# Cross attention: one preparation piece per key tile, keys split bank by bank

## The chip, the cores and the metric

The kernel runs on one core of a Trainium2 chip, as one program. TensorE (PE) multiplies and writes to PSUM, eight banks of 512 f32 columns. VectorE (DVE) and ScalarE (ACT) read PSUM; GpSimd (POOL) works on SBUF; SyncE (SP) issues all DMAs, from one queue in order. Each engine executes its own list of instructions in order, and they wait for each other only at semaphores. The metric is the device time of one execution in microseconds (us). The kernel before took 6407.64 us in the median of three runs (6407.46 to 6416.72).

## The reference

The input is x (32 batches of 100 tokens, 128 wide), a condition vector per batch and a context of 1444 tokens per batch. Four layers follow each other. Layers 0, 1 and 3 are transformer blocks (self attention, cross attention over the context, MLP); layer 2 is a routed mixture without these phases. The change is in the cross attention of layers 0, 1 and 3. In layer 0 the context is normalized first:

```python
q_c = _ln(x) @ W_qc + b_qc
kv_c = _ln(context) @ W_kvc + b_kvc          # layers 1 and 3: context as it is
k_c, v_c = jnp.split(kv_c, 2, axis=-1)
# 16 heads, 8 wide
c_attn_w = jax.nn.softmax(jnp.einsum('bhqd,bhsd->bhqs', q_c, k_c) * scale, axis=-1)
c_attn_out = jnp.einsum('bhqs,bhsd->bhqd', c_attn_w, v_c)
x = x + c_attn_out.transpose(0, 2, 1, 3).reshape(B, N, H) @ W_cproj + b_cproj
```

## The kernel before

`cross_attention_phase` (L934) is a software pipeline over 32 batches. Its unit is a slot: in the slot of batch k, PE computes the scores and the values of batch k, the row maxima of batches k+1 and k+2 and the preparation of batches k+2 and k+3, and the queues carry batches ahead of and behind it. All engines run the same slots, from -3 to 31; slots 1 to 24 are a loop. The order of each engine is written out by hand.

A slot has 12 key tiles, kt 0 to 11, of 128 context tokens (the last has 36). For each key tile PE (`pe_slot`, L1116) does in this order:

- the scores of the tile, two halves of four matmuls (`pe_scores`, L1084, matmul L1093). The queries and keys were split in three bf16 parts, and a row with the negated row maximum is part of the product. ACT turns each half into probabilities (`act_exp`, L1175, activation L1182). A half waits until the exponentials of two halves earlier are done.
- two maxima matmuls (`pe_max`, L1059, matmul L1072) into two banks of the ring; DVE reduces each to one column (`dve_max`, L1216, L1227). There are 48 maxima tiles in a slot, numbered x = 4 kt to 4 kt + 3: the first 32 are for batch k+1, the last 16 for batch k+2.
- the values of the tile before, 16 matmuls of f32 that the trace shows as 32 (`pe_values`, L1097, L1110). The accumulator is copied out once per slot by DVE (`dve_out`, L1253, L1256), after maximum 2.
- two more maxima.
- in kt 8 the turn (`pe_turn_max`, L1075, L1082): the row maxima are transposed, and DVE makes the negated maxima in three parts from them (`dve_negmax`, L1236, L1244 to L1251); SP sends them into the query stack (`sp_negmax`, L1340).
- the preparation pieces that the table `PREPS` (L955) puts in this tile. T0 to T2 transpose the context (L1044), K0 to K2 multiply it with the key weights (L1049), V0 to V2 with the value weights (L1055). Each piece fills one bank, and ACT copies it out (`act_prep`, L1137), behind the exponentials of the same tile: to `ctxT` (L1148), `kf` (L1154), `vals` (L1160, L1165).

Maxima, turn and pieces share a ring of three PSUM banks. `ring_tables` (L913) gives each a place in the order in which PE writes them, and PE waits before it writes to a bank until what was in it has been read (`pe_ring_free`, L1009). One place is left out ahead of the turn and one ahead of maximum 46.

When K2 has been copied, POOL splits the keys in three bf16 parts, with four instructions over all 1444 columns (`pool_split_keys`, L1295, L1302 to L1308). SP then writes the parts to a DRAM stack (`sp_keys_out`, L1349), and two slots ahead of its scores a batch's stack is loaded (`sp_stacks`, L1326). SP's order in a slot is: stack and queries, context (`sp_load_ctx`), sums out (`sp_out`), negated maxima, keys out.

In layer 0 (`normed`) three things are added for batch k+4: DVE takes the statistics of one context tile behind each of the maxima 4 to 15 (`dve_stats`, L1202), aggregates them behind maximum 40 (`dve_aggregate`, L1210) and takes the reciprocal behind maximum 45 (`dve_ctx_rstd`, L1214); ACT takes the square root at the end of kt 10 (`act_ctx_std`, L1173), which needs another table than the exponential; POOL normalizes the context behind the split of the keys (`pool_norm`, L1281).

Of the kernel before, what the change touches and what calls it, by code (L numbers as in the profile page):

```python
# [7 lines left out]
ALU = mybir.AluOpType  # L8
# [5 lines left out]
S = 1444  # L14
# [5 lines left out]
BANK = 512  # L20
# [913 lines left out]
def cross_attention_phase(g, wk, kb, wv, normed):  # L934
# [17 lines left out]
    KW = 16 * 2 * len(K_RUNS)  # L952
    Q_SLOTS = ((0, 3), (3, 2), (5, 1))

    PREPS = {1: ("V0", "V1"), 2: ("V2", "T0"), 3: ("T1", "T2"), 4: ("K0",), 5: ("K1", "K2")}  # L955
    PREP_INDEX = {"T0": 0, "T1": 1, "T2": 2, "K0": 3, "K1": 4, "K2": 5, "V0": 6, "V1": 7, "V2": 8}
    ring_of = lambda kt: ([4 * kt, 4 * kt + 1, 4 * kt + 2, 4 * kt + 3] + (["turn"] if kt == TURN_KT else [])
                          + list(PREPS.get(kt, ())))
# [3 lines left out]
    with ExitStack() as st:  # L962
# [174 lines left out]
        def act_prep(slot, name):  # L1137
            k, i = prep_batch(slot, name), int(name[1])
            if k is None:
                return  # L1140
            b, s, r = k.b, k.s, k.r
            act = g.act
            wait(act, p_full, S1 * b + PREP_INDEX[name] + 1)
            at = bank_of(name)
            if name[0] == "T":
                a = BANK * i
                w = min(BANK, S - a)
                nc.scalar.activation(ctxT[:, a:a + w], ps[:, at:at + w], ACT.Copy).then_inc(p_read, 1)  # L1148
            elif name[0] == "K":
                if i == 0:  # L1150
                    wait(act, parts_ready, b)
                a = BANK * i
                w = min(BANK, S - a)
                nc.scalar.activation(kf[:, a:a + w], ps[:, at:at + w], ACT.Identity, bias=kb).then_inc(p_read, 1)  # L1154
            else:
                k0 = 4 * i
                if i == 0:
                    wait(act, pv_done, KT * (b - LAG + 1))
                full = 4 if i < 2 else 3
                ins = nc.scalar.activation(vals[s][:, k0:k0 + full, :, 0:HD],  # L1160
                                           ps[:, at:at + 128 * full].rearrange("p (k h d) -> p k h d", k=full, h=HEADS),
                                           ACT.Copy)
# [95 lines left out]
        def dve_slot(slot):  # L1258
            before, k1, k4 = slot.k(-1), slot.k(1), slot.k(4)
            for x in range(MT):  # L1260
                dve_max(slot, x)
                if x == 2 and before is not None:
                    dve_out(before)
                if x == MT - MAX_A - 1 and k1 is not None:
                    dve_rowmax(k1)
                if x == 4 * TURN_KT + 3 and k1 is not None:
                    dve_negmax(k1)
                if normed and k4 is not None:
                    if 4 <= x < 4 + KT:
# [22 lines left out]
                nc.gpsimd.tensor_tensor(ctok[s][0:n, last, :], ctok[s][0:n, last, :],  # L1292
                                        column[0:n, last, :].to_broadcast([n, P]), op).then_inc(ctx_ready, 1)

        def pool_split_keys(k):  # L1295

            b, s, r = k.b, k.s, k.r
            pool = g.pool
            wait(pool, p_read, S1 * b + PREP_INDEX["K2"] + 1)
            p = k.prev()  # L1300
            wait(pool, k_written[p.s], KW * (p.r + 1))
            pool_copy(parts[:, 0, :], kf[:, :]).then_inc(split, 1)  # L1302
            wait(pool, split, 3 * b + 1)
            nc.gpsimd.tensor_tensor(kf[:, :], kf[:, :], parts[:, 0, :], ALU.subtract).then_inc(split, 1)  # L1304
            wait(pool, split, 3 * b + 2)
            pool_copy(parts[:, 1, :], kf[:, :]).then_inc(split, 1)
            wait(pool, split, 3 * b + 3)
            nc.gpsimd.tensor_tensor(parts[:, 2, :], kf[:, :], parts[:, 1, :], ALU.subtract).then_inc(parts_ready, 1)  # L1308
# [738 lines left out]
```

## Time and profile before

| what | value |
|---|---|
| median of the runs (lowest, highest) | 6407.64 us (6407.46, 6416.72) |
| profiled execution: time | 6396.8 us |
| profiled execution: span of the core | 6395.0 us |
| mean granted clock of TensorE | 0.866 |
| PE busy over the span | 5146.5 us, 80% |
| PEld (weight loads) | 3314.4 us, 52% |
| DVE | 4097.1 us, 64% |
| ACT | 2978.6 us, 47% |
| POOL | 1581.0 us, 25% |
| maxima L1227 | 2719.1 us busy, 889.9 idle before |
| exponentials L1182 | 1800.9 us busy, 654.2 idle before |

The shares are means over phases with different limits. The execution that was profiled took 6396.8 us, below the lowest of the three timed runs; durations of rows are to be summed against it. Busy time of PE is modelled from the start of matmuls that overlap, so neighbours in the rows overlap. In the rows below, "idle before" in brackets is the time in which the engine had nothing to do before the instruction, and the name behind the arrow is what ended it. A row of the timeline merges neighbours of one kind (xN).

### The profile page before, as it was taken

To read this page: it belongs to the slowest core of one execution; us is meant where nothing else is said; L and a number is where in the kernel's file an instruction comes from. 1 tells how busy PE (TensorE), PEld (TensorE's weight loads), DVE (VectorE), ACT (ScalarE), POOL (GpSimd) and SP (SyncE) were. 2 spreads that over 40 slices of the span, in tenths; PEclk is the share of its full clock that TensorE was granted. 3 is DMA by queue.
4 is the path that set the end of the run, shared out by engine and by line. 5 is a ranking of instruction groups with operands and counts; after the bars stand their busy time and mean duration, and the time that the engine had idled before them with its cause. 6 is when DMAs were issued, how large, how long until landed. Compare 5 with 4: busy or idle time off the path is not lost. (4 is left out here: it accounts for less than half of the span.)

```text
span 6395.0 us, 151199 instructions
## 1 busy us (share of the span) xinstructions
PE 5146.5 (80%) x63886; PEld 3314.4 (52%) x63886; DVE 4097.1 (64%) x7828; ACT 2978.6 (47%) x4342; POOL 1581.0 (25%) x869
## 2 busy tenths in 40 slices
PE   3837999999964839999999757779575699999996
PEld 2614555555542615666666435555352366666663
DVE  5546888888855527777777642324455477777784
ACT  1323666666642315666666522212222366666663
POOL 2024444444312032233222110000301322322221
PEclk7657999999986659999999877769765799999998
DMA  3425555555403434555555111110151555555540
GB/s 72 69 45 161 161 162 162 162 162 162 148 7 63 70 106 156 169 163 162 168 170 171 51 27 51 47 38 1 37 83 28 151 178 168 163 163 172 171 130 15
DMA packets 559421, 726.21 MB, mean 114 GB/s; under 512 B 195354, under 2 KB 471994, under 8 KB 546362
## 3 DMA queue, kind: packets, MB, share of 16 engines
q1 hardware_dynamic: 547226, 701.17, 37.8%
q10 hardware_dynamic: 11520, 15.37, 1.0%
q8 instruction: 505, 8.27, 0.5%
q14 instruction: 170, 1.39, 0.1%
HBM read 450.42 MB, written 264.09 MB: 112 GB/s over the span
## 5 line engine op out<-in xcount | busy, mean ns | idle before, releaser
L1227 DVE TENSOR_REDUCE maxima<-ps 100x1 f32<-100x482 f32 (+1 forms) x4608 | 2719.1, 649 | 889.9 <-PE ps L1072 880.3
L1182 ACT ACTIVATE probs<-ps 128x800 f32<-128x800 f32 (+1 forms) x2304 | 1800.9, 835 | 654.2 <-PE ps L1093 652.5
L1072 PE MATMUL ps<-kst,qst 48*100 48x482 bf16 (+1 forms) x4608 | 1114.3, 410 | 107.9 <-DMA qst<-cross_q_parts 51.5
L1279 POOL TENSOR_TENSOR kparts<-kf,zero 128x1444 bf16<-128x1444 f32 x192 | 498.3, 2595 | 2273.9 <-ACT kf L1154 2243.9
L1110 PE MATMUL ps<-probs,vals 128*9 128x100 f32 x36864 | 1012.5, 250 | 7.9 <-ACT probs L1182 0.8
L1093 PE MATMUL ps<-qst,kst 128*128 128x200 bf16 (+1 forms) x9216 | 999.6, 250 | 10.6 <-DMA qst<-nparts 4.3
L1093 PEld LDWEIGHTS ps<-qst,kst 128*128 128x128 bf16 (+1 forms) x9216 | 759.0, 98 | 250.3 <-issue 124.9
L1110 PEld LDWEIGHTS ps<-probs,vals 128*9 128x9 f32 x36864 | 734.3, 90 | 259.7 <-issue 219.3
L1072 PEld LDWEIGHTS ps<-kst,qst 48*100 48x100 bf16 x4608 | 341.1, 119 | 627.5 <-DVE maxima L1227 328.4
L1160 ACT ACTIVATE vals<-ps 128x512 f32<-128x512 f32 (+1 forms) x288 | 162.1, 563 | 465.8 <-PE ps L1055 465.8
L1044 PE MATMUL ps<-ident,ctok 128*128 128x128 f32 (+1 forms) x1152 | 194.6, 290 | 213.8 <-DMA ctok<-in_ctx_dram 110.1
L711 ACT ACTIVATE probs<-ps 100x800 f32<-100x800 f32 x192 | 159.6, 837 | 368.5 <-PE ps L659 367.5
L1154 ACT ACTIVATE kf<-ps,perm_b_L 128x512 f32<-128x512 f32 (+1 forms) x288 | 190.4, 662 | 285.4 <-PE ps L1049 272.4
L1049 PE MATMUL ps<-ctxT,perm_wk_L 128*128 128x512 f32 (+1 forms) x576 | 288.4, 611 | 39.6 <-DVE maxima L1227 29.5
L723 DVE TENSOR_REDUCE maxima<-ps 100x4 f32<-100x400 f32 x384 | 205.4, 570 | 140.9 <-PE ps L637 140.0
L1304 POOL TENSOR_TENSOR kf<-kf,kparts 128x1444 f32<-128x1444 f32 x96 | 283.2, 2950 | 7.5
L1308 POOL TENSOR_TENSOR kparts<-kf,kparts 128x1444 bf16<-128x1444 f32 x96 | 282.8, 2946 | 7.6
L1044 PEld LDWEIGHTS ps<-ident,ctok 128*128 128x128 f32 (+1 forms) x1152 | 127.0, 143 | 295.7 <-issue 216.3
L1148 ACT ACTIVATE ctxT<-ps 128x512 f32<-128x512 f32 (+1 forms) x288 | 164.7, 572 | 228.8 <-PE ps L1044 225.4
L637 PE MATMUL ps<-kst 96*100 96x100 bf16 x1152 | 143.7, 288 | 152.8 <-DMA kst<-k_parts 124.8
L1055 PE MATMUL ps<-wkv_L,ctxT 128*128 128x128 f32 (+1 forms) x1536 | 217.9, 289 | 32.0 <-DVE maxima L1227 30.5
L1055 PEld LDWEIGHTS ps<-wkv_L,ctxT 128*128 128x128 f32 (+1 forms) x1536 | 181.3, 189 | 76.9 <-DVE maxima L1227 65.6
(251 smaller groups left out, 5193.9 us busy)
## 6 DMA issues: line engine op xcount, KB each, us to landing
kst<-ctx_k_stack SPq DMA_DIRECT2D x96, 2888.0 KB
ctx_k_stack<-kparts SPq DMA_DIRECT2D x192, 541.5 KB
ctx_k_stack<-kparts SPq DMA_DIRECT2D x192, 361.0 KB
ctok<-in_ctx_dram SPq DMA_DIRECT2D x96, 704.0 KB
ctx_k_stack<-kparts SPq DMA_DIRECT2D x192, 180.5 KB
c<-in_ctx_dram SPq DMA_DIRECT2D x32, 704.0 KB
o_sums<-osb SPq DMA_DIRECT2D x96, 200.0 KB
qst<-cross_q_parts SPq DMA_DIRECT2D x1152, 12.5 KB
```

What stands on the lines that cost most here:

```text
L723: nc.vector.tensor_reduce(maxima[:, t // 4, c:c + 4], ps[0:N, at:at + CH].rearrange("p (h k) -> p h k", h=4), AX.X, ALU.max).then_inc(m_re ...
L1044: ins = nc.tensor.transpose(ps[:, at + 128 * q:at + 128 * q + n], ctok[s][0:n, kt, :], g.ident[0:n, 0:n])
L1049: ins = nc.tensor.matmul(ps[:, at:at + w], wk, ctxT[:, a:a + w], start=True, stop=True)
L1055: ins = nc.tensor.matmul(ps[0:n, at + 128 * q:at + 128 * q + 128], ctxT[:, 128 * kt:128 * kt + n], wv, start=True, stop=True)
L1072: nc.tensor.matmul(ps[0:N, at:at + w], g.qst[s][row0:row0 + CROWS, j, N * e:N * e + N], g.kst[s][row0:row0 + CROWS, j, a:a + w], start=Tru ...
L1093: ins = nc.tensor.matmul(ps[0:kts[kt], o:o + 2 * N], g.kst[s][0:KROWS, 4 * hf + jj, 128 * kt:128 * kt + kts[kt]], g.qst[s][0:KROWS, 4 * hf ...
L1110: ins = nc.tensor.matmul(ps[q:q + VW, o:o + N], vals[s][:, kt, h, :], probs[kt % 2][hf][:, N * (2 * jj + e):N * (2 * jj + e) + N], start=( ...
L1182: nc.scalar.activation(probs[kt % 2][hf][0:kts[kt], :].rearrange("p (k n) -> p k n", k=2), src, ACT.Exp).then_inc(exp_done, 1)
L1227: nc.vector.reduce_max(maxima[:, col:col + 1], ps[0:N, at:at + widths[c]], AX.X).then_inc(m_read, 1)
L1279: return nc.gpsimd.tensor_tensor(out, src, g.zero[0:src.shape[0], 0:1].to_broadcast(list(src.shape)), ALU.add)
L1304: nc.gpsimd.tensor_tensor(kf[:, :], kf[:, :], parts[:, 0, :], ALU.subtract).then_inc(split, 1)
L1308: nc.gpsimd.tensor_tensor(parts[:, 2, :], kf[:, :], parts[:, 1, :], ALU.subtract).then_inc(parts_ready, 1)
```

## The change

The table `PREPS` puts one piece in each of kt 0 to 7 and one in kt 9, in the same order V, T, K, so the order in which pieces follow each other on PE and ACT is the same. A constant `STD_KT` of 6 puts the square root of layer 0 at the end of kt 6, the aggregation behind maximum 20 and the reciprocal behind maximum 28. The split of the keys works on one bank (512, 512 and 420 columns) as soon as it is copied: twelve instructions in the place of four. The semaphore counts follow; SP's order stays, and keys go out when all three banks are split.

```diff
@@ cross_attention_phase
-    PREPS = {1: ("V0", "V1"), 2: ("V2", "T0"), 3: ("T1", "T2"), 4: ("K0",), 5: ("K1", "K2")}
+    PREPS = {0: ("V0",), 1: ("V1",), 2: ("V2",), 3: ("T0",), 4: ("T1",), 5: ("T2",), 6: ("K0",), 7: ("K1",), 9: ("K2",)}
+    STD_KT = 6
@@ act_prep, K pieces
-                    wait(act, parts_ready, b)
+                    wait(act, parts_ready, 3 * b)
@@ act_slot
-                if kt == KT - 2 and normed and k4 is not None:
+                if kt == STD_KT and normed and k4 is not None:
                     act_ctx_std(k4)
@@ dve_slot
-                    if x == MT - 8:
+                    if x == 4 * STD_KT - 4:
                         dve_aggregate(k4)
-                    if x == MT - 3:
+                    if x == 4 * STD_KT + 4:
                         dve_ctx_rstd(k4)
@@ pool_split_keys
-        def pool_split_keys(k):
+        def pool_split_keys(k, i):
...
-            wait(pool, p_read, S1 * b + PREP_INDEX["K2"] + 1)
-            p = k.prev()
-            wait(pool, k_written[p.s], KW * (p.r + 1))
-            pool_copy(parts[:, 0, :], kf[:, :]).then_inc(split, 1)
...
+            wait(pool, p_read, S1 * b + PREP_INDEX["K0"] + i + 1)
+            if i == 0:
+                p = k.prev()
+                wait(pool, k_written[p.s], KW * (p.r + 1))
+            a = BANK * i
+            z = min(a + BANK, S)
+            done = 9 * b + 3 * i
+            pool_copy(parts[:, 0, a:z], kf[:, a:z]).then_inc(split, 1)
+            wait(pool, split, done + 1)
+            nc.gpsimd.tensor_tensor(kf[:, a:z], kf[:, a:z], parts[:, 0, a:z], ALU.subtract).then_inc(split, 1)
...
@@ pool_slot
-                pool_split_keys(k3)
+                for i in range(3):
+                    pool_split_keys(k3, i)
@@ sp_keys_out
-            wait(sp, parts_ready, b + 1)
+            wait(sp, parts_ready, 3 * (b + 1))
```

Lines behind the table are numbered one higher in the changed kernel. The first place is PE in layer 0, kt 0 and kt 1 of a slot: L1093 are scores, L1072 maxima, L1110 values, L1055 V pieces. Before:

```order
L1093 MATMUL ps<-qst_11,kst_11 128x200 x8
L1072 MATMUL ps<-kst_11,qst_11 100x480 x2
L1110 MATMUL ps<-probs_90,vals_90 9x100 x16
L1072 MATMUL ps<-kst_11,qst_11 100x482 x2
L1093 MATMUL ps<-qst_11,kst_11 128x200 x8
L1072 MATMUL ps<-kst_11,qst_11 100x482 x2
L1110 MATMUL ps<-probs_90,vals_90 9x100 x16
L1072 MATMUL ps<-kst_11,qst_11 100x480 x2
L1055 MATMUL ps<-wkv_L,ctxT 128x128 x8
```

And after:

```order
L1094 MATMUL ps<-qst_11,kst_11 128x200 x8
L1073 MATMUL ps<-kst_11,qst_11 100x480 x2
L1111 MATMUL ps<-probs_90,vals_90 9x100 x16
L1073 MATMUL ps<-kst_11,qst_11 100x482 x2
L1056 MATMUL ps<-wkv_L,ctxT 128x128 x4
L1094 MATMUL ps<-qst_11,kst_11 128x200 x8
L1073 MATMUL ps<-kst_11,qst_11 100x482 x2
L1111 MATMUL ps<-probs_90,vals_90 9x100 x16
L1073 MATMUL ps<-kst_11,qst_11 100x480 x2
L1056 MATMUL ps<-wkv_L,ctxT 128x128 x4
```

V0 and V1 stood together behind kt 1; now V0 stands behind the last maxima of kt 0 and V1 behind those of kt 1.

The second place is PE behind the turn, kt 9 (L1082 is the turn). Before:

```order
L1082 MATMUL ps<-ident,rowmax 16x100
L1093 MATMUL ps<-qst_11,kst_11 128x200 x8
L1072 MATMUL ps<-kst_11,qst_11 100x480 x2
L1110 MATMUL ps<-probs_90,vals_90 9x100 x16
L1072 MATMUL ps<-kst_11,qst_11 100x482 x2
L1093 MATMUL ps<-qst_11,kst_11 128x200 x8
```

And after:

```order
L1083 MATMUL ps<-ident,rowmax 16x100
L1094 MATMUL ps<-qst_11,kst_11 128x200 x8
L1073 MATMUL ps<-kst_11,qst_11 100x480 x2
L1111 MATMUL ps<-probs_90,vals_90 9x100 x16
L1073 MATMUL ps<-kst_11,qst_11 100x482 x2
L1050 MATMUL ps<-ctxT,perm_wk_L 128x420
L1094 MATMUL ps<-qst_11,kst_11 128x200 x8
```

K2 came from kt 5 to the tile behind the turn.

The third place is ACT in layer 0, from the copy of K0 on (L1154, in kf): L1182 are exponentials, two for each key tile, and L1173 is the square root. Before:

```order
L1154 ACTIVATE kf<-ps,perm_b_L 128x512
L1182 ACTIVATE probs_90<-ps 128x800 x2
L1154 ACTIVATE kf<-ps,perm_b_L 128x512
L1154 ACTIVATE kf<-ps,perm_b_L 128x420
L1182 ACTIVATE probs_90<-ps 128x800 x10
L1173 ACT_TABLE_LOAD
L1173 ACTIVATE rstd<-meanvar,eps 128x12
L1182 ACT_TABLE_LOAD
L1182 ACTIVATE probs_90<-ps 36x800 x2
```

And after:

```order
L1155 ACTIVATE kf<-ps,perm_b_L 128x512
L1174 ACT_TABLE_LOAD
L1174 ACTIVATE rstd<-meanvar,eps 128x12
L1183 ACT_TABLE_LOAD
L1183 ACTIVATE probs_90<-ps 128x800 x2
L1155 ACTIVATE kf<-ps,perm_b_L 128x512
L1183 ACTIVATE probs_90<-ps 128x800 x4
L1155 ACTIVATE kf<-ps,perm_b_L 128x420
L1183 ACTIVATE probs_90<-ps 128x800 x2
L1183 ACTIVATE probs_90<-ps 36x800 x2
```

The square root with its two table loads stood between the exponentials of kt 10 and kt 11; now it stands between the copy of K0 and the exponentials of kt 7.

## Rows read from the trace of the kernel before

**Rows 1.** One line's instructions, L1256, in layers 0 and 1: times, first and last start

```profile
L1256 DVE COPY osb<-ps x28: 562/564/566, 603.4 to 1692.8; 128x400 f32<-128x400 f32 x28
L1256 DVE COPY osb<-ps x29: 562/565/566, 2466.5 to 3542.1; 128x400 f32<-128x400 f32 x29
```

**Rows 2.** Busy time by window, one layer 1 slot: PE, PEld, DVE, ACT, POOL, clock, DMA

```profile
3004.20:3042.60 38.40, 36.50 (x574) 23.92 (x571) 29.56 (x55) 23.78 (x35) 11.10 (x4) 1.00 0.54 169
```

**Rows 3.** Timeline of PE in that slot, from kt 1: start us, us, instruction

```profile
3003.54 0.86 PE L1093 MATMUL ps<-qst,kst 128*128 128x200 bf16 x8
...
3008.42 0.85 PE L1093 MATMUL ps<-qst,kst 128*128 128x200 bf16 x8
...
3012.62 0.85 PE L1093 MATMUL ps<-qst,kst 128*128 128x200 bf16 x8
...
3016.35 0.86 PE L1093 MATMUL ps<-qst,kst 128*128 128x200 bf16 x8
...
3018.86 1.12 PE L1049 MATMUL ps<-ctxT,perm_wk_L 128*128 128x512 f32 x2 [0.17 <-DVE maxima L1227]
3019.83 0.85 PE L1093 MATMUL ps<-qst,kst 128*128 128x200 bf16 x8
...
3024.00 0.85 PE L1093 MATMUL ps<-qst,kst 128*128 128x200 bf16 x8
...
3028.55 0.86 PE L1093 MATMUL ps<-qst,kst 128*128 128x200 bf16 x8
...
3032.15 0.25 PE L1082 MATMUL ps<-ident,rowmax 100*16 100x100 f32 x1 [0.82 <-DVE maxima L1227]
3032.23 0.85 PE L1093 MATMUL ps<-qst,kst 128*128 128x200 bf16 x8
...
3039.67 0.86 PE L1093 MATMUL ps<-qst,kst 128*128 128x200 bf16 x8
```

**Rows 4.** Timeline of DVE in that slot: kt 4, kt 8, behind the negated maxima

```profile
3017.59 2.36 DVE L1227 TENSOR_REDUCE maxima<-ps 100x1 f32<-100x482 f32 x4 [1.38 <-PE ps L1072]
...
3030.21 2.36 DVE L1227 TENSOR_REDUCE maxima<-ps 100x1 f32<-100x482 f32 x4
...
3033.52 6.92 DVE L1227 TENSOR_REDUCE maxima<-ps 100x1 f32<-100x480 f32 x12
```

**Rows 5.** Timeline of PE in slot 29 of layer 1 (no T, no K)

```profile
3546.28 0.85 PE L1093 MATMUL ps<-qst,kst 128*128 128x200 bf16 x8
...
3549.98 0.86 PE L1093 MATMUL ps<-qst,kst 128*128 128x200 bf16 x8
...
3553.64 0.41 PE L1072 MATMUL ps<-kst,qst 48*100 48x482 bf16 x2 [0.52 <-DVE maxima L1227]
```

**Rows 6.** Timeline of DVE in a slot of layer 0: statistics and aggregation

```profile
1013.03 0.28 DVE L1202 BATCH_NORM_STATS2 stats<-ctok 128x6 f32<-128x128 f32 x1
1013.23 0.64 DVE L1227 TENSOR_REDUCE maxima<-ps 100x1 f32<-100x482 f32 x1
...
1039.84 0.80 DVE L1210 BATCH_NORM_AGGREGATE meanvar<-stats 128x2 f32<-128x6 f32 x11
```

**Rows 7.** Timeline of ACT: table loads of layer 0; copy of K0 in layer 1

```profile
1040.07 1.28 ACT L1173 ACT_TABLE_LOAD   x1
...
1042.98 3.09 ACT L1182 ACTIVATE probs<-ps 36x800 f32<-36x800 f32 x4
...
3020.03 0.69 ACT L1154 ACTIVATE kf<-ps,perm_b_L 128x512 f32<-128x512 f32 x1 [1.55 <-PE ps L1049]
```

**Rows 8.** Timeline of PE in layer 0, scores of kt 0

```profile
1043.95 1.15 PE L1093 MATMUL ps<-qst,kst 128*128 128x200 bf16 x8
```

**Rows 9.** Timeline of the layer 1 slot, POOL and SP: last step, keys out

```profile
3033.26 2.95 POOL L1308 TENSOR_TENSOR kparts<-kf,kparts 128x1444 bf16<-128x1444 f32 x1
...
3037.78 5.90 SPq L1355 DMA_DIRECT2D ctx_k_stack<-kparts  x4
```

**Rows 10.** Waits of SP in that slot: us in total, times, longest

```profile
SPq L1347 <- DVE nparts L1251: 3.3, 1, 3.3
```

More of the change, by code:

```diff
@@ L1293, in pool_norm @@
                                         column[0:n, last, :].to_broadcast([n, P]), op).then_inc(ctx_ready, 1)
-        def pool_split_keys(k):
+        def pool_split_keys(k, i):
             b, s, r = k.b, k.s, k.r
             pool = g.pool
-            wait(pool, p_read, S1 * b + PREP_INDEX["K2"] + 1)
-            p = k.prev()
-            wait(pool, k_written[p.s], KW * (p.r + 1))
-            pool_copy(parts[:, 0, :], kf[:, :]).then_inc(split, 1)
[L1303 to L1308, printed above, removed]
+            wait(pool, p_read, S1 * b + PREP_INDEX["K0"] + i + 1)
[8 more added lines that the diff above has]
+            nc.gpsimd.tensor_tensor(kf[:, a:z], kf[:, a:z], parts[:, 0, a:z], ALU.subtract).then_inc(split, 1)
+            wait(pool, split, done + 2)
+            pool_copy(parts[:, 1, a:z], kf[:, a:z]).then_inc(split, 1)
+            wait(pool, split, done + 3)
+            nc.gpsimd.tensor_tensor(parts[:, 2, a:z], kf[:, a:z], parts[:, 1, a:z], ALU.subtract).then_inc(parts_ready, 1)
         def pool_slot(slot):
```

## Prediction

> **What bounds the kernel now.** I read the page first, then the stretches of one slot (a slot is the time in which one batch passes through the scores, 12 key tiles, kt0 to kt11), then the order in time of PE, DVE, ACT, POOL and SP inside one slot. The page's chain ends in the output phase and says nothing of cross attention. But cross attention fills most of the span: the accumulator copy of L1256 runs once per slot, 28 times from 603.4 to 1692.8 us in layer 0 and 29 times from 2466.5 to 3542.1 us in layer 1 [rows 1], so a slot is (1692.8 - 603.4) / 27 = 40.35 us in layer 0 and (3542.1 - 2466.5) / 28 = 38.41 us in layer 1. Layer 3 repeats layer 1. The time of the change is therefore some 84 slots times what it does to one slot, plus the two ends of each phase.
>
> Within a layer 1 slot of 38.40 us PE is busy 36.50, DVE 29.56, ACT 23.78, POOL 11.10, at a granted clock of 1.00, that is 2.4 GHz [rows 2]. PE is the bound, and all that can be won is the 1.9 us between 36.5 and 38.4; DVE (the maxima) makes PE wait at single points, because both share a ring of three PSUM banks. The reader is to see where. I take the start of each group of eight scores matmuls (S) as the beginning of a key tile [rows 3]. From S to S: kt1 4.88 (V0, V1), kt2 4.20 (V2, T0), kt3 3.73 (T1, T2), kt4 3.48 (K0), kt5 4.17 (K1, K2), kt6 and kt7 together 4.55, so 2.28 each without a piece, kt8 3.68 (the turn of the row maxima), and kt9 to kt11 together 7.44, which is 2 x 2.28 + 2.88. What is left for kt0 is 38.40 less 36.13, 2.27.
>
> **One piece alone in a tile.** kt4 is the pattern that the change makes everywhere. It costs 3.48 - 2.28 = 1.20, and only 0.97 of this lies between K0's start and the next S; the other 0.23 is the wait for the ring: K0 takes the bank of the tile's second maximum, and its row names the DVE as releaser [rows 3]. DVE starts 1.24 us after S and reads four tiles in 2.37, 0.58 each [rows 4], so the second is read at 1.24 + 1.17 = 2.41, and K0 starts at 2.51. Two pieces in one tile pay this wait once. So I split each old tile into wait plus work: T0 = (V2 and T0) - (V2 alone). V2 alone stands in the tail slot: 3546.28 to 3549.98, 3.70 [rows 5]; T0 is 4.20 - 3.70 = 0.50. T1 + T2 = 3.73 - 2.28 - 0.23 = 1.22, so 0.50 and 0.72. K1 + K2 = 4.17 - 2.51 = 1.66, K1 as K0 0.97, K2 0.69. V0 + V1: kt1 lasts 4.88, in which DVE comes late from kt0 and the accumulator copy; I value one V piece at 0.95 (V2's 3.70 - 2.51 = 1.19 is an upper end, K0's 0.97 the nearest row).
>
> **Layers 1 and 3, per slot.** After the change: kt0 and kt1 2.51 + 0.95 = 3.46 each; kt2 3.70; kt3, kt4 3.01 each; kt5 3.23; kt6, kt7 3.48 each. kt8: DVE is no longer late when it comes there. Now its four reads start 1.66 after S (3030.21 against 3028.55), since kt6 and kt7 hold no piece and the row maximum comes between; the turn waits for the third of them, S + 1.66 + 1.75 + 0.19 = 3.60 [rows 3, 4]. With 1.24 in the place of 1.66 the turn starts at 3.18 and kt8 is 3.26, a gain of 0.42. kt9: here K2 lands on the one spot where DVE is late: after the turn it does the four steps of the negated maxima and reads again only at 3033.52, 1.37 after the turn [rows 4]; the second read ends at 1.37 + 1.17 = 2.54, K2 starts at 2.65, and S follows at 3.34, so kt9 is 3.34 - 0.08 = 3.26 instead of 2.28. kt10 2.28, kt11 2.88: its two last maxima wait for a skipped place of the ring, which stays. Sum: 6.92 + 3.70 + 6.02 + 3.23 + 6.96 + 3.26 + 3.26 + 2.28 + 2.88 = 38.51, against 38.40: +0.1. By two roundings of a V piece (0.95 or 1.05) it may be +0.3; I take +0.2. In words: eight ring waits of 0.23 and one of 0.3 take the place of five, and this eats the gains at kt8 and kt1. 57 slots (28 each in layers 1 and 3, one of layer 0 without normalization) x 0.2 = +11 us; ends -0.1 and +0.5: -6 and +28.
>
> **Layer 0, per slot.** It has three more costs. (a) The statistics stand behind the maxima of kt1 to kt3; each puts 0.20 between two reads [rows 6]. They now delay V1, V2 and T0 by 0.2 each, 0.6. (b) The aggregation (0.80, L1210 [rows 6]) moves from the maximum 40 to behind 20, so into kt5, and T2 needs the bank of maximum 21: +0.75. (c) The square root of the variance moves on ACT from the end of kt10 to the end of kt6, behind the copy of K0, and it brings two table loads: from 1040.07 to 1042.98, 2.91 us in which ACT makes no probabilities [rows 7]. Now it lies in kt10, followed by the long kt11, and what PE pays for it is seen in the S of kt0, whose eight matmuls take 1.15 [rows 8] instead of 0.86 [rows 3]: 0.29. In kt6 K0 starts at S6 + 2.51 and its copy begins 1.17 later (3018.86, 3020.03) and takes 0.69 [rows 3, 7], so ACT is free at S6 + 4.37 and can start the exponentials of kt7 at S6 + 7.28. S7 is S6 + 3.48, so they start at S7 + 3.80; four take 3.09 [rows 7], two 1.57: done at S7 + 5.37. The second half of the scores of kt8 needs their buffer; it would run at S7 + 3.48 + 0.33 = 3.81. PE loses 1.56. The reciprocal that DVE now waits for in kt7 (maximum 28 is ahead of it) is over before this and hides in it. Sum of layer 0: 38.6 + 0.6 + 0.75 + 1.56 = 41.5, against 40.35: +1.15. (Before, (a) to (c) cost 40.35 - 38.40 = 1.95 together, 0.29 of it ACT's, the rest DVE's.) 27 slots x 1.15 = +31 us; of it +34 is (c), 27 x (1.56 - 0.29). Its ends: wholly hidden, 27 x (0 - 0.29) = -8; wholly on the path, 27 x (2.91 - 0.29) = +71.
>
> The rows on the table loads bear on (c): load, square root, load and exponential follow each other without a gap, 2.91 together [rows 7]. The Trainium skill, page "ScalarE: Activation LUTs", section "What ACT_TABLE_LOAD costs", gives about 2.66 us for each switch, since a drain of 1.38 comes on top of the load; its advice to group functions by table set speaks against this change. By that rule the block is 5.6 us and an exposed one costs 2.7 more per slot; the trace does not agree, its loads of 1.28 us leave no room for a drain.
>
> **Queues and ends.** POOL splits the keys bank by bank. One split is four instructions; the last ends at 3033.26 + 2.95 = 3036.21, 4.06 after the turn, and SP sends the parts at 3037.78, when it is done with the negated maxima [rows 9]. After the change K2 starts at 2.65 after the turn and is copied by about 4.3 (1.17 and at most 0.69 later, 4.5 at the most), and its third of the split takes some 4.0 (four instructions on 420 of 1444 columns, 2.95 x 420 / 1444 = 0.86 each, and an estimated 0.15 of start-up for each), so the parts are ready 8.4 after the turn instead of SP's 5.6. SP's whole chain behind it (key write, stack load, queries, context, sums) is 2.8 us later. SP waits 3.3 us for the next negated maxima now [rows 10], so 0.5 is left; POOL's 11.10 us [rows 2] grow by eight start-ups and stay far under a slot. I cost it at nothing; if the half microsecond is not there, the first scores of a slot wait. At the start of a phase the second batch's K2 comes behind the first maxima, so its keys are out some 9 us later (eight reads of 0.58 and the 4 us of the split): I estimate 0 to 3 us a phase and take 1. At its end tiles without a piece leave a hole in the ring, and the next maxima wait 0.52 [rows 5]; nine tiles have it instead of five: about 1.5 us a phase. Both ends, three phases: +6.
>
> **Sum.** 11 + 31 + 6 = +48; I take +46. The profiled execution has a span of 6395.0 and a time of 6396.8, which gives 6443. The median of the runs shown is 6407.6, 11 above it; the measured median of the new kernel should stand there too: 6407.6 + 46 = 6454.
>
> **Rivals.**
> (1) ACT hides the square root in kt6 as it nearly does in kt10. For it: ACT is busy only 23.78 of 38.4 us [rows 2]. Against: its idle time lies in pieces, as the 1.55 before the copy of K0 [rows 7], and none of them is as long as 2.91. Then (c) is 0.3 and the sum is +46 - 34 = +12: 6420, no change.
> (2) Faster: one piece behind four maxima finds the ring drained, so the 0.23 falls away at all nine places. It decides above a certain size: the sum changes its sign when each wait is shorter by 46 / (84 x 9) = 0.06, that is below 0.17. Wholly gone: 84 x 9 x 0.23 = 174, so 6454 - 174 = 6280. For it: kt6 to kt11 run DVE without a pause today, and spreading gives it back its slack. Against: kt4 is just this case, and waits.
> (3) More than forecast: SP's chain has no half microsecond. Then each slot starts 0.5 to 1 later, 57 x 0.75 = +43: 6497.
> (4) Each of the two switches brings a stall in its new place, where ACT comes from a copy instead of from exponentials. The nearest row for such a stall is the load itself, 1.28 [rows 7]; two of them x 27 = +69: 6523. Against it: no gap stands beside the loads now. This is the drain of the Trainium skill's page "ScalarE: Activation LUTs", section "What ACT_TABLE_LOAD costs".
>
> **Numbers.** Forecast 0.72, (1) 0.11, (2) 0.08, (3) 0.06, (4) 0.03. What a measurement can tell from no change is 0.2%, 13 us: 6395 to 6420. Faster: (2) and a little of the rest, 0.09. Within: (1) and the low end of the forecast, 0.14. Slower 0.77. Range 6418 to 6492: the bounds of layer 0's and the others' slots below and above, without (2) and most of (3) and (4).
>
> **What would show it.** Layer 0's slot 41.3 to 41.7 and the others' 38.4 to 38.8, read from the copies of the accumulator; S to S 3.46 to 3.7 in kt0 to kt2 and 3.0 in kt3 and kt4; kt8 shorter by 0.4, kt9 longer by 1.0; in layer 0 two table loads right behind the copy of K0 and PE waiting for ACT in kt8's scores, 1.5 us; SP still waiting for the negated maxima, by less than 1 us. Wrong if a lone piece starts less than 0.1 behind its maxima, if the load pair stands elsewhere, or if the scores of kt0 wait for a DMA.

## The result and the profile after

The changed kernel took 6457.6 us in the median of four runs (6456.2 to 6461.5), beside 6408.6 (6407.5 to 6416.7) of the kernel before: 1.0075 of the time, 95% interval 1.0057 to 1.0092, or +49 us where +46 was forecast. The two profiled executions stand further apart: 6457.7 (span 6455.9) and 6396.8, 60.9 us. Before's lay 12 below this median, after's lies on its own.

The accumulator copies of layers 0 and 1 (columns as in [rows 1], which they answer):

```profile
L1257 DVE COPY osb<-ps x28: 564/565/566, 606.8 to 1728.0; 128x400 f32<-128x400 f32 x28
L1257 DVE COPY osb<-ps x29: 564/564/567, 2512.2 to 3591.3; 128x400 f32<-128x400 f32 x29
```

Layer 0's slot is (1728.0 - 606.8) / 27 = 41.53 us, 1.18 more. Layer 1's is 38.54; its median is 38.51, 0.11 more, and layer 3's is 38.52. One slot of each layer by windows, the second answering [rows 2]:

```profile
1022.10:1063.70 41.60, 36.73 (x574) 23.93 (x573) 33.23 (x82) 26.25 (x37) 18.35 (x17) 1.00 0.51 156
2974.40:3013.00 38.60, 36.14 (x574) 23.88 (x573) 29.93 (x56) 23.37 (x34) 12.50 (x12) 1.00 0.54 168
```

PE's busy time is no larger than before (36.14 against 36.50) and its clock is at 1.00 in both: what is added is waiting. POOL's twelve instructions take 12.50 where four took 11.10.

PE in that layer 1 slot, from kt 1 (answers [rows 3]; L1094 scores, L1056 V, L1045 T, L1050 K, L1083 turn):

```profile
2974.94 0.85 PE L1094 MATMUL ps<-qst,kst 128*128 128x200 bf16 x8
...
2977.44 1.16 PE L1056 MATMUL ps<-cwv_L,ctxT 128*128 128x128 f32 x8 [0.17 <-DVE maxima L1228]
2978.44 0.85 PE L1094 MATMUL ps<-qst,kst 128*128 128x200 bf16 x8
...
2994.77 0.85 PE L1094 MATMUL ps<-qst,kst 128*128 128x200 bf16 x8
...
2998.23 0.85 PE L1094 MATMUL ps<-qst,kst 128*128 128x200 bf16 x8
...
3001.49 0.85 PE L1094 MATMUL ps<-qst,kst 128*128 128x200 bf16 x8
...
3004.02 0.97 PE L1050 MATMUL ps<-ctxT,perm_wk_L 128*128 128x420 f32 x2 [0.16 <-DVE maxima L1228]
3004.83 0.85 PE L1094 MATMUL ps<-qst,kst 128*128 128x200 bf16 x8
```

From S to S, kt 0 to 11, in the medians of the layer's steady slots: 3.50, 3.50, 3.71, 3.00, 2.99, 3.16, 3.47, 3.47, 3.26, 3.34, 2.27, 2.85. Every piece waits for its bank, as K0 alone did before: V1 2.50 after S (2977.44 - 2974.94), K2 2.53. The two places that were to change most are kt 8, 3.26 (3001.49 - 2998.23) where 3.68 stood, and kt 9, 3.34 (3004.83 - 3001.49, with the turn's matmul 0.09 ahead of S) where 2.31 stood.

Layer 0, ACT and PE from K0's copy in kt 6 into kt 8 (answers [rows 7]):

```profile
1044.03 0.69 ACT L1155 ACTIVATE kf<-ps,perm_b_L 128x512 f32<-128x512 f32 x1 [1.55 <-PE ps L1050]
...
1044.74 1.28 ACT L1174 ACT_TABLE_LOAD   x1
...
1046.36 1.28 ACT L1183 ACT_TABLE_LOAD   x1
1046.37 0.23 DVE L1215 RECIPROCAL rstd<-rstd 128x12 f32<-128x12 f32 x1 [0.66 <-ACT rstd L1174]
...
1047.17 1.12 PE L1050 MATMUL ps<-ctxT,perm_wk_L 128*128 128x512 f32 x2 [1.00 <-DVE maxima L1228]
...
1047.65 1.56 ACT L1183 ACTIVATE probs<-ps 128x800 f32<-128x800 f32 x2
...
1048.55 0.52 PE L1094 MATMUL ps<-qst,kst 128*128 128x200 bf16 x4 [0.25 <-ACT probs L1183]
...
1049.27 0.52 PE L1094 MATMUL ps<-qst,kst 128*128 128x200 bf16 x4 [0.21 <-ACT probs L1183]
```

The block from the first load to the first exponential lasts 1047.65 - 1044.74 = 2.91, as before in its old place. The scores of kt 8 come in two halves with a gap, and from S to S kt 7 and kt 8 take 4.71 + 3.65 = 8.36 instead of the 6.74 that kt 7 and kt 8 would take without it (3.48 + 3.26). Two waits lie in these 1.62 us. DVE stands 0.66 us for the square root, so that K1 waits 1.00 for its bank instead of 0.16; by this alone the scores of kt 8 would start at 1048.13 (K1's 0.96 to the next S behind 1047.17). They start at 1048.55, since ACT's exponentials come later still. The chain through ACT ends last by 0.42, and that through the reciprocal lies inside it.

SP has no wait for the negated maxima left ([rows 10] had 3.3). DVE has them ready at 3002.84 and SP comes to them at 3003.84:

```profile
3002.59 0.25 DVE L1252 TENSOR_TENSOR nparts<-ps,nparts 16x100 bf16<-16x100 f32 x1
...
3003.84 4.12 SPq L1353 DMA_DIRECT2D qst<-nparts  x6
```

The start of a phase, from its first context load to the first accumulator copy, by windows (columns as in [rows 2]); layer 1 of before, then layer 1 of after:

```profile
2330.30:2466.50 136.20, 95.34 (x758) 50.65 (x758) 70.88 (x136) 40.05 (x63) 48.26 (x19) 0.74 0.52 157
```

```profile
2368.50:2512.30 143.80, 101.70 (x754) 53.10 (x755) 71.45 (x136) 39.46 (x62) 53.92 (x51) 0.66 0.48 146
```

The start is 7.6 us longer, and PE is busy 6.4 longer with nearly as many matmuls: its granted clock is 0.66 on the mean instead of 0.74, that is a larger share of the time at 1.2 GHz. Layer 3 gives 7.6 too and layer 0 4.0 (153.1 and 157.1). At the phase's end the tiles without a piece wait, now more of them, in slots 29 and 30 (answers [rows 5]); each of the two is 1.1 to 1.2 longer:

```profile
3626.86 0.86 PE L1094 MATMUL ps<-qst,kst 128*128 128x200 bf16 x8
...
3628.71 0.40 PE L1073 MATMUL ps<-kst,qst 48*100 48x482 bf16 x1 [0.65 <-DVE maxima L1228]
...
3630.19 0.86 PE L1094 MATMUL ps<-qst,kst 128*128 128x200 bf16 x8
```

### The profile page after: what moved, and what is told of

Its sections match the earlier page's. It is cut to its first block and busy times, and to the rows that moved or that the text cites. A ratio compares the mean times of both kernels' runs of the same rounds, so it can differ in the third digit from the quotient of the medians.

```text
span 6455.9 us, 151970 instructions
## 1 busy us (share of the span) xinstructions
PE 5121.1 (79%) x63886; PEld 3304.4 (51%) x63886; DVE 4128.8 (64%) x7828; ACT 2944.9 (46%) x4342; POOL 1715.0 (27%) x1637
## 5 line engine op out<-in xcount | busy, mean ns | idle before, releaser
L1228 DVE TENSOR_REDUCE maxima<-ps 100x1 f32<-100x482 f32 (+1 forms) x4608 | 2748.4, 651 | 899.0 <-PE ps L1073 896.8
L1280 POOL TENSOR_TENSOR kparts<-kf,zero 128x512 bf16<-128x512 f32 (+1 forms) x576 | 569.9, 989 | 2302.7 <-ACT kf L1155 2252.1
L1073 PE MATMUL ps<-kst,qst 48*100 48x482 bf16 (+1 forms) x4608 | 1063.7, 413 | 108.0 <-DMA qst<-cross_q_parts 70.6
L1094 PE MATMUL ps<-qst,kst 128*128 128x200 bf16 (+1 forms) x9216 | 997.4, 250 | 18.9 <-ACT probs L1183 12.9
L1094 PEld LDWEIGHTS ps<-qst,kst 128*128 128x128 bf16 (+1 forms) x9216 | 778.1, 98 | 257.4 <-issue 167.3
L1073 PEld LDWEIGHTS ps<-kst,qst 48*100 48x100 bf16 x4608 | 325.0, 120 | 596.7 <-issue 345.9
L1045 PE MATMUL ps<-ident,ctok 128*128 128x128 f32 (+1 forms) x1152 | 202.0, 294 | 256.6 <-DMA ctok<-in_ctx_dram 110.7
L1050 PE MATMUL ps<-ctxT,perm_wk_L 128*128 128x512 f32 (+1 forms) x576 | 320.2, 641 | 65.9 <-DVE maxima L1228 65.8
L1313 POOL TENSOR_TENSOR kparts<-kf,kparts 128x512 bf16<-128x512 f32 (+1 forms) x288 | 317.8, 1103 | 22.6
L1309 POOL TENSOR_TENSOR kf<-kf,kparts 128x512 f32<-128x512 f32 (+1 forms) x288 | 315.6, 1096 | 22.6
L1045 PEld LDWEIGHTS ps<-ident,ctok 128*128 128x128 f32 (+1 forms) x1152 | 130.1, 146 | 353.4 <-issue 213.3
L1056 PE MATMUL ps<-wkv_L,ctxT 128*128 128x128 f32 (+1 forms) x1536 | 236.0, 295 | 39.7 <-DVE maxima L1228 39.4
L637 PE MATMUL ps<-kst 96*100 96x100 bf16 x1152 | 143.2, 287 | 153.9 <-DMA kst<-k_parts 125.5
L1056 PEld LDWEIGHTS ps<-wkv_L,ctxT 128*128 128x128 f32 (+1 forms) x1536 | 186.9, 190 | 102.3 <-DVE maxima L1228 93.5
```

Of the source, the lines that this page charges most:

```text
L1045: ins = nc.tensor.transpose(ps[:, at + 128 * q:at + 128 * q + n], ctok[s][0:n, kt, :], g.ident[0:n, 0:n])
L1050: ins = nc.tensor.matmul(ps[:, at:at + w], wk, ctxT[:, a:a + w], start=True, stop=True)
L1056: ins = nc.tensor.matmul(ps[0:n, at + 128 * q:at + 128 * q + 128], ctxT[:, 128 * kt:128 * kt + n], wv, start=True, stop=True)
L1073: nc.tensor.matmul(ps[0:N, at:at + w], g.qst[s][row0:row0 + CROWS, j, N * e:N * e + N], g.kst[s][row0:row0 + CROWS, j, a:a + w], start=Tru ...
L1094: ins = nc.tensor.matmul(ps[0:kts[kt], o:o + 2 * N], g.kst[s][0:KROWS, 4 * hf + jj, 128 * kt:128 * kt + kts[kt]], g.qst[s][0:KROWS, 4 * hf ...
L1228: nc.vector.reduce_max(maxima[:, col:col + 1], ps[0:N, at:at + widths[c]], AX.X).then_inc(m_read, 1)
```

## Experiments

Slots are medians over the 27 or 28 steady slots, unless a number is worked out beside it; ratios are to the kernel before, run beside it on the same chip, with their 95% intervals. "After, with" is an edit of the changed kernel.

**e1: after, with the square root, aggregation and reciprocal at their old places.**

```diff
-                if kt == STD_KT and normed and k4 is not None:
+                if kt == KT - 2 and normed and k4 is not None:
-                    if x == 4 * STD_KT - 4:
+                    if x == MT - 8:
-                    if x == 4 * STD_KT + 4:
+                    if x == MT - 3:
```

> The changed kernel with the square root of layer 0 back at the end of kt 10, the aggregation behind maximum 40 and the reciprocal behind maximum 45; one piece per tile and the split by banks stay. Theory (the move of the three costs 1.1 to 1.3 us a slot in layer 0: 0.75 of aggregation in front of T2's bank and 1.6 of table loads in front of kt 7's exponentials, against 1.2 for both at the old place): layer 0's slot falls from 41.5 to 40.3, the others stay at 38.5, the time falls by 27 x 1.2 = 32 us to about 6425. Rival (it is the lone pieces behind the statistics that cost layer 0 its time): the slot stays above 41.2 and the time above 6445.

6444.3 us, 1.0068 [1.0053, 1.0083]. The slots of layer 0 are of two kinds, in turns:

```profile
1012.50:1054.20 41.70, 38.53 (x575) 24.90 (x574) 33.16 (x81) 26.35 (x37) 19.59 (x17) 0.96 0.54 162
1054.20:1094.40 40.20, 36.84 (x571) 23.90 (x571) 33.14 (x82) 26.21 (x37) 17.02 (x17) 1.00 0.49 153
...
1050.00:1054.00 4.00, 3.99 (x46) 2.36 (x45) 1.79 (x4) 1.86 (x3) 3.92 (x3) 0.59 0.97 224
```

At full clock a slot is 40.2 to 40.4, as the sum of the steps had it. But every second slot has a stretch at 0.59 of the clock, from the scores of kt 0 at 1049.61 on, and is 1.5 longer. The whole comes to (1709.5 - 603.9) / 27 = 40.95 by the copies. So the move costs 1.2 at full clock, and half of what undoing it should give back is lost to the clock. That is why the time is 6444 and not the 6425 expected; the rival's slot of 41.2 or more is not there at full clock.

**e2: before, with only the moves of the square root, aggregation and reciprocal.**

```diff
-                if kt == KT - 2 and normed and k4 is not None:
+                if kt == 6 and normed and k4 is not None:
-                    if x == MT - 8:
+                    if x == 20:
-                    if x == MT - 3:
+                    if x == 28:
```

> The kernel before with nothing but the move: square root at the end of kt 6, aggregation behind maximum 20, reciprocal behind maximum 28. No K0 copy stands ahead of the table loads here, so ACT comes to them 2.2 us earlier after the scores of kt 6, but kt 6 is also 1.2 shorter. Theory: exponentials of kt 7 end at S7 + 4.3, PE loses 1.7; aggregation 0.75 in kt 5 ahead of K1's bank; kt 8 gains 0.4 since DVE catches up, and 1.2 fall away in kt 11 and kt 0: layer 0's slot 40.35 + 0.8 = 41.2, time 6408 + 22 = 6430. Rival (kt 7 without a piece has room for it): slot 40.3 or less, time at or below 6408.

6469.6 us, 1.0109 [1.0094, 1.0124]: slower than the whole change. The theory had 6430 and the rival 6408 or less, so both missed the time. Layers 1 and 3 stay at 38.40; in layer 0 one slot of three is 41.4 and the others 44:

```profile
994.90:1036.30 41.40, 36.37 (x573) 23.75 (x571) 32.67 (x81) 26.48 (x38) 16.82 (x8) 1.00 0.45 143
1036.30:1080.40 44.10, 39.06 (x573) 25.16 (x571) 33.06 (x82) 26.56 (x38) 16.80 (x8) 0.92 0.52 160
...
1060.30:1064.30 4.00, 2.43 (x45) 1.36 (x43) 3.42 (x8) 3.96 (x6) 3.84 (x3) 1.00 0.09 20
...
1068.30:1072.30 4.00, 4.00 (x46) 2.42 (x45) 2.35 (x7) 1.57 (x2) 4.00 (x3) 0.52 0.02 5
```

What PE did ahead of the fall:

```profile
1055.92 1.83 PE L1049 MATMUL ps<-ctxT,perm_wk_L 128*128 128x512 f32 x4 [0.96 <-DVE maxima L1227]
...
1063.67 0.52 PE L1093 MATMUL ps<-qst,kst 128*128 128x200 bf16 x4 [1.46 <-ACT probs L1182]
```

The undisturbed slot is the 41.2 that was expected, within 0.3. The rest is the clock, which falls after these two waits and 2.43 us of work in 4.

**e9: after, with the square root at the end of kt 8, the reciprocal behind maximum 36.**

```diff
-                if kt == STD_KT and normed and k4 is not None:
+                if kt == TURN_KT and normed and k4 is not None:
-                    if x == 4 * STD_KT + 4:
+                    if x == 4 * TURN_KT + 4:
```

> The changed kernel with the square root two tiles later, at the end of kt 8, and the reciprocal behind maximum 36; the aggregation stays behind maximum 20. This parts the two costs of the move: the table loads (1.6) should be hidden, since the turn and K2 make kt 8 and kt 9 long enough for ACT, and the aggregation ahead of T2's bank (0.75) stays. Layer 0's slot 41.5 - 1.6 + 0.2 (the reciprocal ahead of K2's bank) = 40.1, time 6458 - 27 x 1.4 = 6420. If the loads cost PE as much wherever they stand, 41.5 and 6458.

6411.8 us, 1.0017 [1.0008, 1.0026]. Only the two loads and the reciprocal moved, and the slot goes from 41.53 to (1683.7 - 604.8) / 27 = 39.96, at full clock:

```profile
1004.50:1044.40 39.90, 36.25 (x573) 23.93 (x572) 33.00 (x81) 26.22 (x37) 18.18 (x17) 1.00 0.53 162
```

That is 1.57 per slot. The block is as long as ever there:

```profile
1031.98 1.28 ACT L1174 ACT_TABLE_LOAD   x1
...
1034.89 1.56 ACT L1183 ACTIVATE probs<-ps 128x800 f32<-128x800 f32 x2
```

2.91 again (1034.89 - 1031.98). What differs is how much of it PE feels: next to nothing here (kt 7 and kt 8 are back at 3.46 and 3.25, kt 9 is 0.09 longer), 1.6 behind kt 6, where kt 7 follows at once. This shows step (c) of the prediction apart from (a) and (b). It takes away the wait for ACT and that of DVE for the square root together; that ACT's is the one that sets the 1.6 is read from the rows of kt 7 and kt 8 above.

**e4: before, with the pieces between the second value product and the last two maxima; e3: the same on e1.**

```diff
-    ring_of = lambda kt: ([4 * kt, 4 * kt + 1, 4 * kt + 2, 4 * kt + 3] + (["turn"] if kt == TURN_KT else [])
-                          + list(PREPS.get(kt, ())))
+    ring_of = lambda kt: ([4 * kt, 4 * kt + 1] + list(PREPS.get(kt, ())) + [4 * kt + 2, 4 * kt + 3]
+                          + (["turn"] if kt == TURN_KT else []))
@@ pe_slot
+                for name in PREPS.get(kt, ()):
+                    pe_prep(slot, name)
                 pe_max(slot, 4 * kt + 2)
                 pe_max(slot, 4 * kt + 3)
                 if kt == TURN_KT:
                     pe_turn_max(slot)
-                for name in PREPS.get(kt, ()):
-                    pe_prep(slot, name)
```

> The kernel before with nothing but the pieces between the values and the second pair of maxima (two pieces in a tile as before, keys split whole, K2 in kt 5). Theory: five ring waits of 0.23 and the lateness in kt 1 go, 1.3 to 1.8 us a slot; the second half of the slot (kt 6 to 11 without pieces, DVE without a pause, turn at 3.6) stays; K2 in kt 5 lets the keys out early, so SP's queue holds a slot of 36.7: layer 1's slot 36.7 to 37.1, layer 0's 38.6 to 39.0, time 6408 - 84 x 1.5 = 6280. Rival (the third-next maximum now waits for ACT's copy of the piece): slot 38 or more, PE waits for ACT in L1072.

> The changed kernel, square root and aggregation at their old places, and the piece of a tile stands between the values and the second pair of maxima, in the ring too, so that it takes the bank of the tile before's last maximum, long read. Theory of the ring wait (0.23 at each lone piece, 0.3 at K2): eight or nine waits go, 2.1 us a slot; layer 1 would have 38.5 - 2.1 = 36.4. But SP's queue in the changed kernel has hardly any slack (its negated maxima start 0.9 after they are ready), and a slot of 36.4 is shorter than its chain from the last third of the split to the next negated maxima; with both, layer 1's slot ends between 36.4 and 38.5, PE waits for the DMA of the negated maxima in kt 0. If only the ring waits counted: 36.4 and 37.6 in layer 0, time about 6230. If ring waits are only renamed (PE waits for DVE elsewhere): slot at 38.5, time 6425.

e4: 6333.1 us, 0.9899 [0.9882, 0.9915]; e3: 6347.7, 0.9919 [0.9904, 0.9934]. The layer 1 slot goes to 37.81 and 37.68, by 0.6 and 0.8, less than half of what I expected of e4. A piece no longer waits, but the maxima behind it do, inside their row:

```profile
2927.69 1.27 PE L1055 MATMUL ps<-cwv_L,ctxT 128*128 128x128 f32 x8
2928.90 0.66 PE L1044 MATMUL ps<-ident,ctok 128*128 128x128 f32 x4
2929.48 0.62 PE L1072 MATMUL ps<-kst,qst 48*100 48x482 bf16 x2
2930.04 0.86 PE L1093 MATMUL ps<-qst,kst 128*128 128x200 bf16 x8
```

These rows are e4's. A pair of maxima takes 0.41 where it doesn't wait, and 0.62 here. With two pieces per tile the wait moves on to the pair; with one (e3) the pair behind a piece takes 0.40 to 0.41. But e3 loses elsewhere: its nine tiles with a piece are 1.3 shorter together than e1's, and kt 8 goes from 3.26 back to 3.69, the length it had in before. So its 36.4 of ring waits alone is far off, and 6347.7 lies between its two ends (6230 and 6425). The ring wait is real, and moving the piece ahead of it gives 0.6 to 0.8 a slot, where spreading the pieces gave nothing.

**e7: e4, with the skipped place ahead of V0 in the place of maximum 46.**

```diff
-    skips=("turn", 46)
+    skips=("turn", "V0")
```

> The kernel before with the pieces between values and second maxima, and with the ring place that is left out ahead of maximum 46 left out ahead of V0 instead. Theory: the last maximum of kt 11 no longer waits 0.56 for the one two before it, while V0's bank has long been read: slot 37.8 to 37.3 in layers 1 and 3, 39.0 to 38.3 in layer 0; 6333 - 42 = 6291. Rival (DVE is the bound from kt 6 to kt 11, so the wait only moves to kt 0): slot unchanged, 6333.

6332.1 us, 0.9885 [0.9868, 0.9901], not to be told from e4. The layer 1 slot gains 0.2 (37.60), layer 0 loses 0.3 (39.33), and the 6291 of the theory is missed. In layer 1 kt 11 falls from 2.85 to 2.29, the 0.56 that I expected, but kt 1 grows from 4.42 to 4.75: the wait moves, as the rival had it, and reappears in kt 1.

**e5: after, with K1 and K2 both in kt 7.** It was to explain the longer start of the phases: theory A put it down to K2's late place, theory B to the clock alone.

```diff
-    PREPS = {..., 6: ("K0",), 7: ("K1",), 9: ("K2",)}
+    PREPS = {..., 6: ("K0",), 7: ("K1", "K2")}
```

> The changed kernel with K2 behind K1 in kt 7 in the place of kt 9; nothing else. In a steady slot it takes away the wait of K2 behind the negated maxima (kt 9 3.35 to 2.28, kt 7 3.47 to 4.17): 38.5 to 38.1, 84 x 0.35 = 29 us. Also K2 then stands ahead of the first maxima of the next batch, so at the start of a phase the second batch's keys go out some 12 us earlier. Theory A (the start of a phase is 3 to 8 us longer because K2 stands behind the maxima that wait for the stack): the first copy of the accumulator in layers 0, 1 and 3 comes as early as before, 15 us more: 6458 - 44 = 6414 in all. Theory B (it is longer because lone pieces and waits keep PE at 1.2 GHz up to the first scores, where before it ran a part at 2.4 GHz): the start stays as it is, granted clock 0.50 up to the first scores, 6429.

6411.5 us, 1.0010 [1.0000, 1.0019]. The slots fall to 40.62 and 38.18: 0.34 by one shared wait, and in layer 0 0.57 more. There kt 7 and kt 8 are 5.00 and 3.48, 0.83 and 0.22 above layer 1's, so the square root costs 1.05 in the place of 1.62: K1 still waits 1.00 behind the reciprocal, and K2's work fills most of the time in which PE waited for ACT. The time is the 6414 of theory A and not the 6429 of B, but by this 0.57 a slot (27 x 0.57 = 15 us), which neither had. Theory A falls in the main, since the start stays long:

```profile
2342.40:2483.80 141.40, 100.41 (x754) 52.83 (x755) 71.07 (x136) 39.56 (x62) 53.94 (x51) 0.69 0.49 149
```

It is 141.4 at a clock of 0.69, where before has 136.2 at 0.74 and after 143.8 at 0.66. e7, with before's `PREPS`, has 135.8 at 0.74. The same instructions take either length with the clock, as layers 1 and 3 of e2 show, whose starts are before's:

```profile
2404.60:2540.80 136.20, 95.24 (x758) 50.66 (x758) 70.83 (x135) 40.00 (x63) 48.32 (x19) 0.74 0.52 157
5043.60:5183.90 140.30, 100.86 (x758) 51.67 (x758) 70.89 (x136) 41.33 (x64) 48.36 (x19) 0.70 0.50 152
```

So a lower clock lengthens a start by itself, here by 4.1. Whether it is all of the 7.6, no run shows, and why the clock is low there is open: e4 has 142.6 at 0.68 in layer 1 with before's `PREPS`, so the spread pieces are not needed for it.

**e6: after, with the keys split whole, once K2 is copied.** One split of four instructions, one count per batch in the place of three.

```diff
-                for i in range(3):
-                    pool_split_keys(k3, i)
+                pool_split_keys(k3)
@@ sp_keys_out
-            wait(sp, parts_ready, 3 * (b + 1))
+            wait(sp, parts_ready, b + 1)
```

> The changed kernel with the keys split whole, by four instructions after K2's copy, as before; K2 stays in kt 9. The parts are then ready 4.3 + 11.3 = 15.7 after the turn instead of 8.3. Theory (SP's queue is the next bound: 32.6 us lie between the first key write and the next negated maxima, whose landing opens the next slot 30.0 ahead of the next turn): 2 x slot = 15.7 + 32.6 + 6.0 + 30.0 = 84.3, slot 42.2 in layers 1 and 3, 43.6 in layer 0, time 6458 + 57 x 3.7 + 27 x 2.1 = 6725. If the queue has slack for it, slot 38.5 and time 6458.

6880.1 us, 1.0747 [1.0719, 1.0774], slower than either theory had it (6725 and 6458). SP's waits in one layer 1 slot (us, times, longest), SP's queries, and PE behind kt 8's scores, in kt 9 and at the next slot's start:

```profile
SPq L1356 <- POOL kparts L1309: 9.2, 1, 9.2
```

```profile
3141.58 8.35 SPq L1338 DMA_DIRECT2D qst<-cross_q_parts  x12
...
3153.15 0.41 PE L1073 MATMUL ps<-kst,qst 48*100 48x482 bf16 x2 [2.47 <-issue]
...
3155.62 1.41 PE L1094 MATMUL ps<-qst,kst 128*128 128x200 bf16 x8
...
3166.71 0.86 PE L1094 MATMUL ps<-qst,kst 128*128 128x200 bf16 x8 [1.33 <-DMA qst<-nparts]
```

SP stands 9.2 us behind a split that starts only when K2 is there, and all that it sends behind the keys comes late; the slot's median is 44.3 us in layer 1 and 44.6 in layer 3. PE stands idle for 2.47 us ahead of the first maxima of kt 8. The trace names no releaser, but these are the first tile of batch k+2, before which `pe_max` waits for that batch's stack and queries, and SP had sent the last of them just before. The scores of the next kt 0 wait 1.33 for the negated maxima. PE loses clock too: the eight scores of kt 9 take 1.41 instead of 0.85. So the split by banks is what makes K2 in kt 9 bearable. In the changed kernel SP waits 1.7 us for it.

**e8 and e11: what the others pointed to.** e8 is e1 with e4's order of pieces, e7's skip and e5's place of K2. e11 is the same with e9's place of the square root.

> One piece per tile with K1 and K2 in kt 7, split by banks, pieces between values and second maxima, the left out place ahead of V0, square root and aggregation at their old places. K2 early frees SP (parts ready 6 after the turn), and DVE is not late at the turn. By the sums of the theory: 36.4 + 0.1 for each of nine pieces - 0.56 = 36.7 in layers 1 and 3, 38.0 in layer 0, time near 6408 - 57 x 1.7 - 27 x 2.3 + 15 for the starts and ends = 6265. If SP's queue binds (its own work and landings are 35 to 36 us a slot and grow with contention): 37.5 and 6300.

> The best version so far with the aggregation behind maximum 20, the square root at the end of kt 8 and the reciprocal behind maximum 36. With the pieces ahead of the second maxima no piece waits for the maximum behind the aggregation. Layer 0's slot 39.2 - 1.1 = 38.1, the others 37.0, time 6306 - 30 = 6276. If DVE's 33 us a slot bind in layer 0, it stays above 39 and 6300.

e8: 6305.9 us, 0.9842 [0.9827, 0.9856]; e11: 6291.0 us, 0.9825 [0.9809, 0.9841]. Both beat both kernels. Their layer 1 slots are alike, 36.98 and 36.97:

```profile
2889.70:2926.70 37.00, 36.10 (x573) 23.68 (x571) 29.70 (x56) 24.34 (x35) 12.46 (x12) 1.00 0.57 175
```

PE is busy 36.10 of 37.0: 0.9 us is left of the 1.9 that stood open in [rows 2]. Layer 0 is 39.23 in e8 and 38.74 in e11. Both are slower than their sums had it (6265 and 36.7 for e8, 6276 and 38.1 in layer 0 for e11).

**e10: the changed kernel once more.**

> The changed kernel once more, unaltered, for the spread between executions and for the starts of the phases: slot 41.5, 38.5, 38.5; granted clock 0.50 from the first maxima to the first scores of layer 1 if that belongs to its pattern (then first copy 659 us after layer 0's last), otherwise shorter in this execution. Time 6450 to 6460.

6457.0 us, 1.0085 [1.0070, 1.0100]; slots 41.52 and 38.51, starts 156.7, 143.3 and 143.2. So the starts of after are long in two executions, not by chance in one. Beside its own thirteen runs of before (median 6401.7) the difference is +55 us, where the first comparison gave +49; the two intervals overlap.

## Why the prediction came out

The forecast of +46 was met by +49 of the medians (+55 in e10), and the mechanism of the slots, point by point, held:

- **A lone piece pays the ring wait.** Forecast 3.46, 3.46, 3.70, 3.01, 3.01, 3.23, 3.48, 3.48 for kt 0 to 7; all measured within 0.07. The rounding of a V piece lay between 0.95 and 1.05, nearly 1.0. e3 and e4 show the wait from the other side. Rival (2) fell; what it would have given (6280) is nearly what e11 gets, by other means.
- **kt 8 and kt 9.** Forecast 3.26 and 3.26; measured 3.26 and 3.34. Nine ring waits for five, less the turn's 0.42 and what kt 1 gains, give +0.11 a slot, beside +0.1 of the sum and the +0.2 that I took: 57 x 0.12 = 6.8 us instead of 11.
- **Layer 0's three costs.** Forecast 41.5, measured 41.53; 27 x 1.18 = 31.8 us instead of 31. One by one: the statistics 0.19 in each of kt 1 to 3 (forecast 0.20), the aggregation 0.79 in kt 5 (0.75), the loads 1.62 in kt 7 and 8 (1.56) and 1.57 by e9. That the reciprocal hides in ACT's delay held too, by 0.42. Rival (1) fell, since ACT hid little of it in kt 6, and rival (4) too, since no gap stands beside the loads in any place.
- **SP's queue.** The half microsecond that I left it isn't there: SP comes 1.0 after the negated maxima. Yet rival (3) did not follow, no slot grew by it. The step was mis-costed in the chain and right in the time: in the layer 1 slot shown, no wait of PE names a DMA. What SP sends isn't needed that soon in a slot of 38.5; e6, where the chain is later still, shows what it looks like when it is.
- **The ends are the term that was mis-sized.** I had +6 for three phases; my own terms, 1 and 1.5 us a phase, give 7.5. The starts measure 4.0 + 7.6 + 7.6 = +19.2 (forecast 3) and the ends, two slots of some +1.15 in each of three phases, +7 (forecast 4.5). I counted the late K2 and did not look at the clock of the start, where before already runs at 0.72 to 0.74.

Of the 60.9 between the profiled executions that is 31.8 + 6.8 + 19.2 + 7 = 64.8, and layer 2 and the rest are some 4 shorter. So the nearness of +46 and +49 is in part luck: the slots give 39 of forecast 42, starts and ends 20 more than forecast, and the profiled execution of before that I compared with was 12 below its median while after's isn't. I also took +46 where my terms add up to 48, without a reason. That the distance to the median carries over from one kernel to the next was an assumption, and it failed.

The table switch was the one dispute with the Trainium skill. In kt 6, kt 8 and kt 10 the block is 2.91 each time, with loads of 1.28. The Trainium skill, page "ScalarE: Activation LUTs", section "What ACT_TABLE_LOAD costs", adds a drain of 1.38 to each switch; no run here shows one. The advice of that page of the Trainium skill, to do the functions of one table set together, bears on a place where a switch is exposed (1.6 us in kt 6) and not on one where it is hidden (kt 8 of e9).

## What to carry to other kernels

Where two engines share a small ring of buffers, spreading small jobs evenly is not a gain by itself: each job that stands alone pays the wait for the ring, and two together pay it once, so look first at whose read the job waits for, and move it ahead of that. A switch of ACT's table costs what the next consumer feels of it: 0, 0.3 or 1.6 us of the same 2.9, by the place in the slot. Undoing a costly step does not give its whole price back if the clock takes part of it, so read the granted clock of a slot beside its length.

## What the hardware showed that I had not expected

- The granted clock of TensorE falls inside steady slots. In e1 it stands at 0.59 over 4 us, from scores in kt 0 before which PE was idle 0.21, in e2 at 0.52 (1.2 GHz all but throughout) after waits of 0.96 and 1.46, in e6 at 0.89 over a whole slot. After itself has the same 1.6 of ACT's delay in every layer 0 slot, and its clock is 1.00. What makes the difference no run here isolates.
- In the start of a phase after works at 1.2 GHz from 2416 to 2475, some 59 us in one piece, with PE busy 14.56 us of 15 in one of the windows. Up to 2416 it was at 1.2 GHz too, with PE busy 0.03 of the 26 us from 2390. At 2475 the clock is back:

```profile
2416.00:2430.00 14.00, 11.42 (x24) 3.36 (x25) 11.20 (x20) 0.61 (x1) 3.73 (x4) 0.50 0.16 39
2430.00:2445.00 15.00, 14.56 (x47) 7.74 (x46) 9.41 (x17) 2.44 (x5) 0.00 (x0) 0.50 0.83 263
...
2475.00:2490.00 15.00, 14.21 (x237) 9.70 (x235) 10.84 (x19) 9.07 (x15) 0.00 (x0) 0.98 0.76 267
```

- Cutting POOL's four instructions into twelve adds 1.4 us a slot (12.50 against 11.10), 0.18 for each of the eight more; my estimate of 0.15 was near.
